# Weighing of an attention step on TensorE: two halves of 256 queries, or all 512 queries at once

## What is computed

```
x = x + retention(layernorm(x))          # 4 heads, chunked decay
x = x + channel_mix(layernorm(x))
x = x + attention(layernorm(x))          # 16 heads of 16, relative position bias
x = x + channel_mix(layernorm(x))

# attention, per sequence:
scores = einsum('bhqd,bhkd->bhqk', q, k) / sqrt(16) + bias[None]
attn   = softmax(scores, axis=-1)
out    = einsum('bhqk,bhkd->bhqd', attn, v)      # then @ wo.T + bo
```

## Time and profile before

| | us |
|---|---|
| median of 3 runs (3419.11 to 3433.25) | 3419.49 |
| the profiled execution, its own time | 3418.34 |
| its span, first to last instruction | 3416.3 |
| TensorE busy / mean granted clock | 3060.4 (90%) / 0.92 |
| VectorE, ScalarE, GpSimd busy | 2046.2, 1730.9, 1228.1 |
| row maxima on VectorE (L1272), 1024 of them | 1235.5 |
| exponentials on ScalarE (L1029), 2048 of them | 1114.2 |
| weighing on TensorE (L652), 8192 matmul instructions | 651.6 |

### The profile page before, as it was taken

The page is one execution under the profiler, slowest core; times in us unless marked ns, Lnnn a source line. Parts: engine busy times, 40 slices in busy tenths (PEclk is TensorE's granted clock), DMA queues, the critical chain, the costliest instruction groups (busy, mean ns, idle before and its releaser), DMA issues.

```text
span 3416.3 us, 50321 instructions
## 1 busy us (share of the span) xinstructions
PE 3060.4 (90%) x18786; PEld 1621.7 (47%) x18786; DVE 2046.2 (60%) x3247; ACT 1730.9 (51%) x3667; POOL 1228.1 (36%) x1748
## 2 busy tenths in 40 slices
PE   6969999699996999879998899978999789997898
PEld 3634466244663446534465344653446534564344
DVE  4448644586445854468544785447854478444783
ACT  2427743287342763338633376333763348532575
POOL 2314533154331543315432244322443224432343
PEclk8969999699996999969999699996999879998799
DMA  5050000600005000140002400023000330003200
GB/s 147 13 123 2 2 13 16 120 2 1 13 25 111 2 1 13 48 88 2 1 13 58 78 2 1 13 65 72 2 4 10 73 64 2 7 7 73 52 2 13
DMA packets 54898, 115.88 MB, mean 34 GB/s; under 512 B 10480, under 2 KB 33056, under 8 KB 54528
## 3 DMA queue, kind: packets, MB, share of 16 engines
q1 hardware_dynamic: 54656, 112.67, 14.9%
HBM read 69.24 MB, written 45.11 MB: 33 GB/s over the span
## 4 chain that ended last, share of the span: by engine, by line
PE 73%; DMA 9%; DVE 7%; issue 4%; POOL 3%; ACT 3%; SPq 1%; POOLq 0%; DVEq 0%; ACTq 0%
PE psum L600 18%; PE psum L652 17%; PE psum L496 9%; PE psum L629 9%; DMA SQ<-mrow 4%; PE psum L703 3%; DMA parts<-Z 3%; PE psum L515 2%; DVE mx L1272 2%; DMA SK<-parts 2%; PE psum L744 2%; PE psum L684 2%; PE psum L730 2%; PE psum L747 1%; POOL X L1363 1%
## 5 line engine op out<-in xcount | busy, mean ns | idle before, releaser
L1272 DVE TENSOR_REDUCE mx<-psum 128x1 f32<-128x1024 f32 x1024 | 1235.5, 1222 | 406.0 <-PE psum L600 405.6
L1029 ACT ACTIVATE Z<-psum 128x512 f32<-128x512 f32 x2048 | 1114.2, 597 | 469.4 <-PE psum L629 429.2
L1445 POOL TENSOR_TENSOR Z<-Z,band_exp 128x256 f32<-128x256 f32 (+1 forms) x1152 | 714.4, 642 | 1219.5 <-ACT Z L1029 1212.2
L629 PE MATMUL psum<-SQ,SK 64*128 64x512 f32 x2048 | 883.3, 480 | 98.4 <-DMA SQ<-mrow 98.4
L600 PE MATMUL psum<-SK,SQ 63*128 63x512 f32 x2048 | 844.9, 503 | 138.0 <-DMA SK<-parts 114.5
L652 PE MATMUL psum<-Z,Vx 128*17 128x256 f32 x8192 | 651.6, 393 | 0.0
L600 PEld LDWEIGHTS psum<-SK,SQ 63*128 63x128 f32 x2048 | 349.0, 212 | 574.2 <-issue 272.5
L629 PEld LDWEIGHTS psum<-SQ,SK 64*128 64x128 f32 x2048 | 367.8, 189 | 295.5 <-ACT Z L1029 179.3
L496 PE MATMUL psum<-Wqkvg,Z 128*128 128x512 f32 x768 | 371.3, 609 | 18.5 <-ACT Z L936 18.5
L652 PEld LDWEIGHTS psum<-Z,Vx 128*17 128x17 f32 x8192 | 140.4, 96 | 293.4 <-issue 278.8
L496 PEld LDWEIGHTS psum<-Wqkvg,Z 128*128 128x128 f32 x768 | 137.4, 190 | 144.1 <-issue 110.3
(11 more groups left out here) (121 smaller groups left out, 3312.9 us busy)
## 6 DMA issues: line engine op xcount, KB each, us to landing
parts<-Z SPq DMA_DIRECT2D x48, 512.0 KB
SQ<-parts SPq DMA_DIRECT2D x48, 256.0 KB, 8.7
SK<-parts SPq DMA_DIRECT2D x48, 256.0 KB, 11.6
Xin<-L_attn_a_x SPq DMA_DIRECT2D x8, 1024.0 KB, 5.4
parts<-mixed SPq DMA_DIRECT2D x16, 512.0 KB
SQ<-parts SPq DMA_DIRECT2D x16, 512.0 KB, 8.2
SK<-parts SPq DMA_DIRECT2D x16, 512.0 KB, 13.6
out<-X SPq DMA_DIRECT2D x16, 512.0 KB, 3.0
```

The costliest lines, as they stand in the source:

```text
L629: pe.matmul(col_bank(s, i), SK[rows_of(h), h // 2, j * P:j * P + P], SQ[rows_of(h), h // 2, 512 * half:512 * half + 512], start=True, stop ...
L1029: nc.scalar.activation(ring[:, n % RING, :], col_bank(s, i), ACT.Exp)\
L1272: nc.vector.tensor_reduce(mx[:, blk, col:col + 1], bank_pair[u % 2], AX_X, ALU.max)\
L1445: nc.gpsimd.tensor_tensor(ring[:, n % RING, a:z], ring[:, n % RING, a:z], band_exp[:, 4 * hg + COLS[i], at:at + z - a], ALU.mult)\
```

## The change

`weigh` loses its `part` argument and covers all 512 queries with one call of four matmuls. It is called once in a step, where the first half was; the call behind the second pair of scores is gone. The waits of the first half stay where they are, and the semaphore `e_pv`, which the second half raised, is now raised by the only one. The number of columns that are multiplied, the banks, the ring and all other engines' programs stay as they are. In the trace of before a fp32 matmul stands as two instructions, so a half is 8 of them with 256 columns each; a whole would be 8 with 512.

```diff
-            def weigh(b, s, part):
+            def weigh(b, s):
 
                 hg, half, j = step(s)
-                if part == 0:
-                    if bands[s]:
-                        need(pe, e_band, b, 4 * banded[s])
-                    else:
-                        need(pe, e_p, b, 4 * s + 4)
-                    if s % 8 == 0:
-                        need(pe, mx_row, b, s // 8 + 1)
-                cols = slice(256 * part, 256 * part + 256)
+                if bands[s]:
+                    need(pe, e_band, b, 4 * banded[s])
+                else:
+                    need(pe, e_p, b, 4 * s + 4)
+                if s % 8 == 0:
+                    need(pe, mx_row, b, s // 8 + 1)
                 for c in range(4):
-                    mm = pe.matmul(sum_bank(s // 8)[32 * c:32 * c + HD + 1, cols], Vx[:, j, 4 * hg + c, :],
-                                   ring[:, (4 * s + COLS.index(c)) % RING, cols],
-                                   start=s % 8 == 0 and part == 0, stop=s % 8 == 7, skip_group_check=True)
-                if part == 1:
-                    mm.then_inc(e_pv.sem, 1)
+                    mm = pe.matmul(sum_bank(s // 8)[32 * c:32 * c + HD + 1, :], Vx[:, j, 4 * hg + c, :],
+                                   ring[:, (4 * s + COLS.index(c)) % RING, :],
+                                   start=s % 8 == 0, stop=s % 8 == 7, skip_group_check=True)
+                mm.then_inc(e_pv.sem, 1)
...
                     if s >= LAG:
-                        weigh(b, s - LAG, 0)
+                        weigh(b, s - LAG)
                     if s < NS:
                         for k in range(2):
                             if u + 1 < NU:
                                 score_rows(b, u + 1, k)
                             score_cols(b, s, 2 + k)
-                    if s >= LAG:
-                        weigh(b, s - LAG, 1)
```

## The result

| | us |
|---|---|
| kernel before, median of 4 | 3420.39 |
| changed kernel, median of 4 (3519.56 to 3526.11) | 3521.18 |
| ratio | 1.029, 95% interval 1.026 to 1.032 |

The change costs 101 us, 2.9%. I forecast 118 (3538, range 3485 to 3595). On the page TensorE's busy share falls from 90% to 87% of a longer span, and ScalarE appears in the chain that ended last with its exponentials (L1024; the lines behind the diff have moved up by three to five). Before, no exponential of the scores stood in that chain: the largest entries are in the earlier trace rows, and it isn't among the smaller ones either.

A forecast was written before the change was run, and what follows sets the result against it. The bound was a once-per-step loop through TensorE and ScalarE over two banks. Per sequence 15.8 - 1.5 + 0.5 = 14.8 us, 118 for eight, gave 3536.7, about 3538 us on the median's scale; range 3485 to 3595.

The forecast's parts named there:

- The bound: A plain step is a 2.73 us loop through TensorE and ScalarE over two banks, closed at the second score pair.
- The sign that was named for the change: The first score pair's weight load waits for ScalarE once a step, about half a microsecond.
- W = 0.98: The whole weighing on TensorE takes 0.98 us until the next score, 0.43 more than a half.
- Both bounds, 0.85 and 1.12: Limits for the whole weighing: 0.85 us if the fixed 0.13 went, 1.12 if it were two halves in a row.
- The new step, 3.15: A plain two-bank step takes 0.60 + 0.65 + 0.49 + 0.43 + 0.98 = 3.15 us against 2.73.
- Transposes hidden between B and A: Transposes, about 0.75 us per eight steps, fit TensorE's wait between the second score pair and the next step's first.
- WIDE and projections, -1.5: Four-bank steps 53 to 59 gain 1.9 us; with handing over and projection steps 60 to 63, -1.5 per sequence.
- The first weighings, +0.5: Steps 2 to 4, low clock: the clock rises in the step after the first weighing; +0.5 us per sequence.
- The end, 0: Between projection and layernorm transposes, losses in steps 62 and 63 are covered by VectorE and GpSimd's chain: 0 us.
- The gain from fewer turns: Rival, 7%: bank waits don't bind and fewer turns between scores and weighing make the kernel faster, 3302 us.
- The loss was not half as large: Rival, 6%: bank 4 frees sooner or the second score needn't follow by 0.49; 0.2 a step lost, 3467 us.
- The clock didn't fall: Rival, 3%: TensorE's pauses drop the clock in narrow steps; a step takes 4.4 us, in all about 4050.

The follow-up runs named there:

- The V of the splits: Kernel before with its weighing split unevenly: 384 queries behind the first score pair and 128 behind the second, 3453.93 us; 128 and 384, 3510.12 us.
- the four cells of banks and merging: Full-clock steps in the kernel before and kernels with row scores ahead: two banks 2.71 us halves, 3.08 whole; four banks 2.43 halves, 1.82 to 2.8 whole.
- the 288/224 split: Kernel before with 288 queries of weighing behind the first score pair and 224 behind the second: 3402.93 us, ratio 0.994.
- ahead_2_whole: Kernel before with all 128 units of row scores run ahead, two banks in all steps, whole weighing behind the first score pair: 4957.52 us.

## Why the prediction was right, and where it was off

*The bound.* Right: a step is set by a loop through TensorE and ScalarE over two banks and not by TensorE's own work, though TensorE showed no gap. The wait of 0.23 at B was the sign of it. The V of the splits and the four cells of banks and merging show it, and so does the 288/224 split, which shortens the step to 2.67 with the work of every engine as before. The sign that was named for the change is there: the weight load of A's first score waits for ScalarE once a step, 0.66 at 295.79.

*W = 0.98.* Right to 0.01 wherever a whole weighing is shown above, and it was read from the low-clock half: twice the columns at twice the clock. Both bounds, 0.85 and 1.12, are excluded; the second by the two halves in a row, which also take 0.99.

*The new step, 3.15.* Measured 3.09. Of its five terms 0.65, 0.49, 0.43 and 0.98 hold to 0.01; the first, 0.60, is 0.54. I took A's value for B, and B's own was in the trace of before, where ScalarE stands idle before B (step 3, B's first score and its exponential):

```profile
251.51 0.49 PE L629 MATMUL psum<-SQ,SK 64*128 64x512 f32 x1
...
252.05 1.09 ACT L1029 ACTIVATE Z<-psum 128x512 f32<-128x512 f32 x2 [0.58 <-PE psum L629]
```

Six hundredths on 48 steps are 2.9 us per sequence, 23 in all: more than the whole miss of 17.

*Transposes hidden between B and A.* Right: 24.70 for eight steps is 8 x 3.09, so nothing is left of the 0.75.

*WIDE and projections, -1.5.* Measured -1.45, by other parts. I had 1.9 gained in seven WIDE steps and 0.4 given back at the ends. The seven gained only 0.87 (16.95 against 17.82), since step 59, whose next A is back on two banks, takes 2.82 where it took 2.43; steps 60 and 61 gained 0.57, where the forecast had them only in the 0.4 given back. ScalarE became the engine that the scores wait for, as told, but not at 2.16 a step: eight exponentials take 4.03, 2.0 a step, and waits at the transposes and for the maxima come on top. The sum agreed by luck.

*The first weighings, +0.5.* Measured +1.30. I let the clock rise in the next step always. In three sequences the profiled execution had a second step at the low clock, which is 0.55 of the missing 0.8; 0.8 us on eight sequences is 6 us, which took back part of the 23. That the two misses have opposite signs is luck.

*The end, 0.* Right: from the projection's start to the layernorm transposes it is 11.05 us before and 11.04 after, with 1.93 idle where 1.91 was:

```profile
429.85 3.72 PE L681 MATMUL psum<-WT,Z 128*128 128x256 f32 x16
...
440.89 1.94 PE L506 MATMUL psum<-ident,nrm 128*128 128x128 f32 x8 [1.93 <-issue]
```

*The rivals.* The gain from fewer turns exists, 16.95 against 17.82 in the WIDE steps, but only where the bank waits don't bind. The loss was not half as large, since bank 4 came free after 0.65 and A's second score followed by 0.49, as taken from the trace of before (the 6 us per sequence of that rival aren't worked out in the prediction). The clock didn't fall in the narrow steps (1.00 from 255 to 404 us); of its price, a step of 4.4 at the low clock was taken, and ahead_2_whole has 4.53. The prediction calls the stretch from 239 to 251 us one without weighing; its last part has the first weighing, at 246.37.

Of the rules of the Trainium skill, the one that decides the narrow steps is that groups should rotate through banks so that emptying one overlaps the next ("Perfetto Trace Analysis", Matmuls); giving up that overlap cost 101 us here. The same section's rule that larger matmuls are more efficient than smaller ones doesn't show: two halves in a row take 0.99 and a whole 0.98. That weight loads overlap only with matmuls in other rows (the Trainium skill, "TensorE: Matmul & The Clock Gate", The mechanism) speaks for fewer turns, which is what the WIDE steps gained by, but no run here shows that rule by itself.

## What to carry to other kernels

An engine without a gap in the trace can still be waiting in a loop: look for the small wait that comes back once per step, and write the loop down as a sum. Work that can be placed freely is cover for round trips, and merging two pieces of it uncovers one unless there are buffers enough; if it can be cut unevenly, write the sum for each trip and set the cut where the two meet. In this kernel merging paid in the steps that have the spare banks or other work (the projections) in the gap, and lost in the narrow ones.

## What the runs showed of the hardware that was not expected

The clock. With halves and without row scores TensorE showed 100.00 of 100.00 us busy and stayed at 0.50 (1.2 GHz) through all 60 steps, in all eight sequences, on two banks and on four, at 4.27 us a step. With the same columns merged into one weighing on four banks it stood at 1.00 after three or four steps in every sequence (in one of them it fell once, for two steps). Merged on two banks it rose at different steps: after some ten steps in the first sequence (4.53 a step, then 3.08), where it even showed less busy time (43.25 of 46.00) before the rise; in the others after 12, 36 or 44 steps, and in two of the eight not before the projections. All eight run the same program ahead of these steps. The kernel before does the same steps with halves at 1.00 in its WIDE stretch, but it comes there at the full clock. So shown busy time doesn't tell whether the clock will rise, and the same steps can run at either level; what decides it no run here shows. Between the two kernels on four banks, which differ by the merging alone, nearly all of the 1017 us is this; a change measured in a kernel that sits at the low clock says little of one that doesn't.
